# A mixture of experts on one core: token tiles of 128 rows of one expert, or of two halves of 64 rows with an expert each

## What is computed

```python
x = layernorm(x + attention(x, w_qkv, w_out))          # x: (4, 512, 256)
w, idx = top_k(softmax(x @ gate), 4); w = w / w.sum()  # gate: (256, 32)
gate_up = einsum('TD,EDF->TEF', x, gate_up_proj)       # 32 experts, (256, 192) each
g, u = split(gate_up, 2)
y = einsum('TEF,EFD->TED', u * silu(g), down_proj)     # (96, 256) each
x = layernorm(x + (y * router_weights).sum(experts))   # only the 4 chosen count
```

## Time and profile before

| | us |
|---|---|
| median of 3 runs | 473.64 (470.53 to 474.44) |
| the profiled execution | 470.53, its span 468.8 |
| PE busy | 401.1 (86%) |
| DVE, ACT, POOL busy | 281.8, 245.8, 244.0 |
| expert stage on PE | from 283.95 to 428.55 |

### The profile page before, as it was taken

One profiled execution on the slowest core, in us unless ns is written; L12 is line 12 of the kernel. 1 busy time (PEld: TensorE's weight loads), 2 busy tenths in 40 slices (PEclk: granted clock), 3 DMA queues, 4 the chain that ended last, 5 costly groups with the idle time before them and its releaser, 6 DMA issues.

```text
span 468.8 us, 9779 instructions
## 1 busy us (share of the span) xinstructions
PE 401.1 (86%) x2613; PEld 268.1 (57%) x2613; DVE 281.8 (60%) x835; ACT 245.8 (52%) x594; POOL 244.0 (52%) x362
## 2 busy tenths in 40 slices
PE   5755899999988899978988717979999999996692
PEld 2422565455564356544544416859889998984240
DVE  1225774787459985899797394534555555551295
ACT  1412265676454676558757143544666666654054
POOL 4301242533332387635874737777777667765341
PEclk9989899999999999999999876998999999999697
DMA  4689473385467157497557249979755556300993
GB/s 161 148 173 174 125 130 88 92 147 100 108 186 143 27 105 163 131 215 193 172 157 212 93 138 300 286 229 307 205 162 176 155 169 171 110 3 4 395 383 116
DMA packets 55795, 76.77 MB, mean 164 GB/s; under 512 B 9650, under 2 KB 47804, under 8 KB 54208
## 3 DMA queue, kind: packets, MB, share of 16 engines
q1 hardware_dynamic: 48112, 59.22, 49.0%
q0 software_dynamic: 7632, 16.93, 10.1%
HBM read 46.23 MB, written 33.75 MB: 171 GB/s over the span
## 4 chain that ended last, share of the span: by engine, by line
PE 56%; DVE 17%; DMA 9%; SPq 6%; issue 6%; POOL 4%; ACT 1%; ACTq 0%; DVEq 0%; POOLq 0%
PE PS L730 11%; PE PS L746 7%; PE PS L602 6%; PE PS L535 6%; PE PS L559 5%; DVE MX L989 5%; PE PS L581 4%; PE PS L717 4%; SPq L495 3%; POOL scratch_slots L1300 2%; DMA scratch_qk<-PA 2%; PE PS L546 2%; PE PS L563 2%; PE PS L740 2%; PE PS L660 2%
## 5 line engine op out<-in xcount | busy, mean ns | idle before, releaser
L845 ACT ACTIVATE PT<-PS 128x512 f32<-128x512 f32 x160 | 92.9, 596 | 49.2 <-PE PS L581 44.2
L1307 POOL DMA_INDIRECT scratch_y<-Y,XG x95 | 93.6, 985 | 36.8 <-ACT Y L899 25.1
L989 DVE TENSOR_REDUCE MX<-PS 128x1 f32<-128x384 f32 (+1 forms) x192 | 88.5, 503 | 37.1 <-PE PS L563 37.0
L1283 POOL TENSOR_SCALAR_AFFINE_SELECT PT<-PT 128x256 f32<-128x256 f32 (+1 forms) x140 | 50.9, 372 | 75.9 <-ACT PT L845 74.0
L1300 POOL DMA_INDIRECT scratch_slots<-XP,RI x64 | 63.1, 986 | 35.9 <-DVE XP L1118 19.0
L730 PE MATMUL PS<-W,XGT 128*128 x380 | 80.5, 336 | 0.3 <-DVE XGT L1204 0.2
L559 PE MATMUL PS<-KS,QS 96*128 96x512 bf16 (+3 forms) x256 | 61.6, 303 | 21.1 <-DVE MX L989 12.5
L730 PEld LDWEIGHTS PS<-W,XGT 128*128 128x128 f32 x380 | 61.8, 196 | 1.0 <-issue 0.9
L581 PE MATMUL PS<-QS,KS 98*128 98x512 bf16 (+3 forms) x256 | 60.9, 299 | 1.4 <-ACT PT L845 1.4
L1211 DVE SCALAR_TENSOR_TENSOR HH<-PS,XG,SG 128x96 f32<-128x96 f32 x95 | 30.2, 318 | 52.5 <-ACT SG L887 52.0
L746 PE MATMUL PS<-W,HT 96*128 x190 | 57.3, 383 | 0.0
(11 more groups left out here) (169 smaller groups left out, 552.9 us busy)
## 6 DMA issues: line engine op xcount, KB each, us to landing
XG<-scratch_slots SPq DMA_DIRECT2D x95, 130.0 KB, 2.7
YL<-scratch_y SPq DMA_DIRECT2D x16, 512.0 KB, 10.7
scratch_qk<-PA SPq DMA_DIRECT2D x48, 128.0 KB
KS<-scratch_qk SPq DMA_DIRECT2D x48, 128.0 KB, 7.2
W<-_L_ffn_gate_up_proj_dram SPq DMA_DIRECT2D x16, 288.0 KB, 3.6
scratch_slots<-pad SPq DMA_DIRECT2D x33, 130.0 KB, 7.4
QS<-scratch_qk SPq DMA_DIRECT2D x8, 384.0 KB, 5.0
W<-in_L_ffn_down_proj_dram SPq DMA_DIRECT2D x8, 288.0 KB, 5.6
```

Of the source, the lines that this page charges most:

```text
L845: e.activation(PT[:, p % NPT, n, :], PS[:, 2 + (rank[u] - 1) % 2, :], ACT.Exp).then_inc(st_exp, 1)
L989: t = e.tensor_reduce(M[:, h, qt:qt + 1], PS[:, kk, c0:c0 + w], AX.X, ALU.max)
L1283: e.affine_select(out=d, in_=d, compare_op=ALU.is_ge, fill=0.0, base=0, pattern=[[0, 1 if n < 2 else 2], [1, 128]], channel_multiplier=-1) ...
L1307: e.indirect_dma_start(out=YK[:, :], out_offset=bass.IndirectOffsetOnAxis(ap=XG[:, j % NXG, D + 1:D + 2].bitcast(I32), axis=0), in_=Y[:, j ...
```

## The change

A tile now has two halves of 64 slots, each with an expert of its own. The first half uses columns 0 to 63 of the array and writes PSUM partitions 0 to 63, the second half the other 64. An expert's rows are rounded up to 64, and the count becomes `TILES` = (8192/64 + 32)/2 = 80, with `EARLY` = 32. The first half's weights are still addressed in `W` by a register. Those of the second half are copied into two fixed rings: DVE copies gate and up (384 columns) into `WG`, ACT the down weights (256 columns) into `WD`. Both engines read the expert's place from the table for it. SP loads a tile with two DMAs of 64 rows and reads two tables. The fills have 64 rows. They are cut into groups of four, and behind each group stand three or two early tile loads. PE no longer drains its pipeline between early and late tiles: `experts` is one loop, and the wait for the late table moves into it. The tables lie in `WOT`, whose first content is dead by then. Row blocks of `X` are normalised on every second tile instead of every fourth.

```diff
-TILES = B * S * TOPK // 128 + NE - 1
+HALF = 64
+TILES = (B * S * TOPK // HALF + NE) // 2
-EARLY = -(-((B - 1) * S * TOPK - 127 * NE) // 128)
+EARLY = -(-((B - 1) * S * TOPK - (HALF - 1) * NE) // HALF) // 2
+FILLS = 4
...
-    plan += [("early",)]
+    plan += [("early", 0, 8)]
     plan += [("rows", B - 1, q, k) for q in range(2) for k in range(TOPK)]
-    plan += [("fill",)]
+    tile = 8
+    for n in range(0, NE, FILLS):
+        step = 3 if n < NE // 2 else 2
+        plan += [("fill", n), ("early", tile, tile + step)]
+        tile += step
+    plan.append(("early", tile, EARLY))
...
-                e.dma_start(XG[:, j % NXG, :], XS[bass.ds(slot[j], 128), :]).then_inc(xg_in[j % NXG], 16)
+                for n in range(2):
+                    if j in row_starts:
+                        slot.update(zip([(t, n) for t in row_starts[j]],
+                                        row_values(mybir.EngineType.SP, table_piece(0, n, row_starts[j]))))
+                    e.dma_start(XG[HALF * n:HALF * n + HALF, j % NXG, :],
+                                XS[bass.ds(slot[j, n], HALF), :]).then_inc(xg_in[j % NXG], 16)
...
             def stage_b(j):
                 if j >= 2:
                     e.wait_ge(hh_out, j - 1)
                 e.wait_ge(xgt_out, j + 1)
+                e.wait_ge(wg_out, j + 1)
                 for c in range(2):
-                    t = e.matmul(PS[:, 2 + j % 2, 0:2 * FF], XGT[:, j % 2, c, :],
-                                 W[:, bass.ds(reg[j] + 2 * FF * c, 2 * FF)], start=(c == 0), stop=(c == 1))
+                    e.matmul(PS[0:HALF, 2 + j % 2, 0:2 * FF], XGT[:, j % 2, c, 0:HALF],
+                             W[:, bass.ds(reg[j] + 2 * FF * c, 2 * FF)], start=(c == 0), stop=(c == 1))
+                    t = e.matmul(PS[HALF:128, 2 + j % 2, 0:2 * FF], XGT[:, j % 2, c, HALF:128],
+                                 WG[:, j % 2, 2 * FF * c:2 * FF * c + 2 * FF], start=(c == 0), stop=(c == 1))
...
-                e.matmul(PS[:, 6 + j % 2, 0:D], HT[:, j % 2, :], W[0:FF, bass.ds(reg[j] + 4 * FF, D)],
+                e.wait_ge(wd_out, j + 1)
+                e.matmul(PS[0:HALF, 6 + j % 2, 0:D], HT[:, j % 2, 0:HALF], W[0:FF, bass.ds(reg[j] + 4 * FF, D)],
+                         start=True, stop=True)
+                e.matmul(PS[HALF:128, 6 + j % 2, 0:D], HT[:, j % 2, HALF:128], WD[0:FF, j % 2, :],
                          start=True, stop=True).then_inc(y_full, 1)
...
+            def copy_down(j):
+
+                if j == EARLY:
+                    e.wait_ge(tile_at, 3)
+                if j in row_starts:
+                    reg.update(zip(row_starts[j], row_values(mybir.EngineType.Activation,
+                                                             table_piece(1, 1, row_starts[j]), (NE - 1) * WROW)))
+                if j >= 2:
+                    e.wait_ge(y_full, j - 1)
+                e.activation(WD[0:FF, j % 2, :], W[0:FF, bass.ds(reg[j] + 4 * FF, D)], ACT.Copy).then_inc(wd_out, 1)
...
-            to_normalise = {EARLY + 8 + 4 * t: t for t in range(NT)}
+            to_normalise = {EARLY + 8 + 2 * t: t for t in range(NT)}
...
+            def copy_up(j):
...
+                if j >= 2:
+                    e.wait_ge(gu_full, j - 1)
+                e.tensor_copy(WG[:, j % 2, :], W[:, bass.ds(reg[j], 4 * FF)]).then_inc(wg_out, 1)
+
+            def experts():
+                copy_up(0)
+                for i in range(TILES + 1):
+                    if i < TILES:
+                        stage_a(i)
+                    if i:
+                        stage_b(i - 1)
+                    if i + 1 < TILES:
+                        copy_up(i + 1)
```

More of the change, by code:

```diff
@@ L390, in build, with table_piece, by_half @@
                       for lo in range(first, end, TOGETHER)}
-        def table_piece(row, tiles):
-            table, first = (ETI, 0) if tiles[0] < EARLY else (TI, EARLY)
-            return table[row:row + 1, tiles[0] - first:tiles[-1] + 1 - first]
+        def table_piece(row, half, tiles):
+            table, first, n = (ETI, 0, EARLY) if tiles[0] < EARLY else (TI, EARLY, TILES - EARLY)
+            at = half * n - first
+            return table[row:row + 1, at + tiles[0]:at + tiles[-1] + 1]
+        def by_half(table):
+            return table.rearrange("p (n j) -> p j n", n=2)
         def row_values(engine, row, most=NE * CAP):
@@ L483, in _ @@
                 elif kind == "early":
[L484 to L488, removed]
+                    lo, hi = a
+                    if lo == 0:
+                        e.wait_ge(*free(("etable",)))
+                        for q in range(4):
+                            wait_rows(e, B - 1, q)
+                        wait_pv(e, PAIRS - 1)
+                    for j in range(lo, hi):
                         load_tile(j)
                 elif kind == "fill":
+                    n, = a
                     e.wait_ge(fill_at, 1)
                     wait_const(e, "pad")
-                    for n in range(0, NE, 4):
-                        for v in row_values(mybir.EngineType.SP, FI[0:1, n:n + 4]):
-                            e.dma_start(XS[bass.ds(v, 128), :], pad[:, :]).then_inc(fill_out, 16)
+                    for v in row_values(mybir.EngineType.SP, FI[0:1, n:n + FILLS]):
+                        e.dma_start(XS[bass.ds(v, HALF), :], pad[0:HALF, :]).then_inc(fill_out, 16)
             e.wait_ge(tile_at, 3)
@@ L1213, in stage_b, with experts @@
                                        op1=ALU.mult).then_inc(hh_out, 1)
[L1215 to L1217 removed]
+            reg = {}
+            def copy_up(j):
+                if j == EARLY:
+                    e.wait_ge(tile_at, 3)
+                if j in row_starts:
+                    reg.update(zip(row_starts[j], row_values(mybir.EngineType.DVE, table_piece(1, 1, row_starts[j]),
+                                                             (NE - 1) * WROW)))
+                if j >= 2:
+                    e.wait_ge(gu_full, j - 1)
+                e.tensor_copy(WG[:, j % 2, :], W[:, bass.ds(reg[j], 4 * FF)]).then_inc(wg_out, 1)
+            def experts():
+                copy_up(0)
+                for i in range(TILES + 1):
+                    if i < TILES:
                         stage_a(i)
[L1219 removed]
+                    if i:
                         stage_b(i - 1)
[L1222 to L1223 removed]
+                    if i + 1 < TILES:
+                        copy_up(i + 1)
+            e.wait_ge(*free(("etable",)))
+            e.wait_ge(w_in, 48 * kinds["w"])
+            experts()
             for t in range(0, NT + 2, 2):
```

75 lines of the change are left out of this document (36 added, 39 removed).

## The result

The changed kernel takes **505.78 us** (median of 4 runs, 505.55 to 506.04) against 473.28 us before (4 runs on the same chip): ratio 1.0696, 95% interval 1.0649 to 1.0743. The forecast was 484, its range 472 to 500. Slower is right, and so is the main reason, but the time is 22 us over the forecast and outside the range. The profiled execution is one of 505.85 us with a span of 504.0. (In the prediction, rows 10 and 11 are cited the wrong way round: the landing time is in rows 10, POOL's first scatter in rows 11.)

A forecast was written before the change was run, and what follows sets the result against it. The expert stage was taken as bound by columns streamed through PE's array. Tiles -21.2, gap and second start -5.65, visits +37.9 gave +11.0 us on the median 473.64: 484.6, given as 484, range 472 to 500.

The forecast's parts named there:

- The tiles removed: On PE in the expert stage: fifteen tiles fewer at 1.416 us each, 21.2 us saved.
- the halves run side by side: Stages b and d on PE: column strips run together, so a pair of halves costs the price of one.
- the rival of 571 us: Stages b and d on PE: halves run one after the other, +1.08 us a tile, 86 us in all; chance 0.02.
- The switch is not free: Against the rival on PE that switching costs nothing for halves of 64: period 1.42, 453 to 465 us, chance 0.16.
- The copies are hidden: Weight copies on DVE and ACT: done an iteration before PE needs them, costed at nothing.
- DVE and ACT keep up: Per tile, DVE needs at most 1.38 us and ACT 1.28 to 1.58, plus 0.07 each, under PE's 1.89.
- the second start of the pipeline: PE between early and late tiles: one loop removes the 2.05 us gap and 3.6 for a second start, 5.65 together.
- the new period is 1.416 + 0.47 = 1.89 us: PE, per tile: two visits to column tiles at 0.235 us each added to the old period; 37.9 us in 80 tiles.
- weights are not hidden: Rival on PE: each of six passages a tile exposes 0.06 us, 0.36 a tile, 29 us; 490 to 515 us, chance 0.10.
- so nothing waits: SP's queue: at 0.58 us a load and 0.665 a fill, rows land before PE wants them, so the 5.65 us are gained.
- The margin of 10 us: Tile 17's rows: landed by 310 us, wanted by PE at 320.
- the test itself: Sign of error: PE waiting for DMAs of XG between 300 and 340 us would mean SP binds.

The follow-up runs named there:

- experiment 1: The kernel before with its 95 tiles, only stages b and d cut into two column tiles of 64, nothing copied: 549.51 us against 518.0.
- experiment 5: The changed kernel with the fills issued by ACT, 128 rows each, so that SP only loads tiles: 487.97 us, ratio 1.0388 to the kernel before.
- the pairs: The changed kernel with two tiles per visit and fills on ACT's queue: ratio 0.9889; with c and d two tiles later still, 462.64 us, ratio 0.9832.
- experiment 4: The changed kernel with c ahead of b, one visit per tile: 513.89 us, ratio 0.9970; with tiles loaded before fills as well, 483.42 us, ratio 1.0270.
- experiment 2: The kernel before with each tile load of 128 rows cut into two DMAs of 64: 529.43 us against 518.0, ratio 1.0288.

## Why the prediction missed

**Right.** The tiles removed are worth 1.416 us each and the halves run side by side (the rival of 571 us is out). The switch is not free: 0.095 us on entry into stage b and 0.101 on exit, where the forecast had 0.097. The copies are hidden: experiment 1 has the same period without them. DVE and ACT keep up; the second start of the pipeline is gone. With what the forecast left out taken away, its own sum comes back: experiment 5 gives a stage of 164.0 us against 155.6, and 8.6 of the difference are the period's.

**The step "the new period is 1.416 + 0.47 = 1.89 us"** has the right mechanism and too small a size. The price of a visit was read from strips of 32 columns: 0.235, of which 0.194 are entry and exit and 0.041 the rest. At full clock the median steps of one tile are longer than before by 0.095 us into stage b, 0.049 from its first record to its second, 0.101 out of it, 0.135 into d, 0.047 inside d, 0.102 out of it, and 0.052 from a's first transpose to its second. These are all of the 0.581 us. So the rest is about 0.05 twice in a visit: from its first record to its second, and behind the first full-width matmul after it (for c, which has only one, it shows as 0.135 instead of 0.095). Three orders of PE give the same price: (1.997 - 1.416)/2 = 0.290, 1.713 - 1.416 = 0.297, and 2 x (1.560 - 1.416) = 0.288 us per visit. The forecast had 0.235. That is 8.6 us in 80 tiles. The rival "weights are not hidden" was right in kind at most for the first record and not for every passage: the later steps in stage b are 0.162 us, in the pairs too, as before. The measured time lies in its band of 490 to 515, but for another reason: it asked for 0.36 us a tile beyond the forecast, and there are 0.107. The Trainium skill (TensorE: Matmul & The Clock Gate, LDWEIGHTS) gives a load as its columns over 1.2 GHz, 53 ns for 64; the 0.047 to 0.049 inside a visit are near it, and the later passages, at 0.162, show no such load. By this rule of the Trainium skill, as an estimate, 128 columns would be 107 ns and 96 columns 80, while the step behind a visit is 0.052 with 128 and 0.040 with 96. So that the two steps are exposed weights is plausible but not shown. (That loads overlap matmuls only for another row group, as the forecast quotes, the page says under The mechanism, and the steps of 0.162 between matmuls on the same 128 rows do not bear it out.)

**The step "so nothing waits"** failed. It took 0.58 us for a load of 64 rows from a row of loads with 128 rows. The record is 0.469 us instead of 0.333, and with the tables' reads a DMA took 0.81 on average, so tile 17 came 8 us later than forecast. It also put all 4.4 us of the stage's start and draining ahead of the tiles, while TensorE took the first 17 tiles in 34.0 us and stood at tile 17 at 315.9 instead of 320. The margin of 10 us became a wait of 2.5. The forecast had drawn up the test itself (a wait for `XG` between 300 and 340: SP binds), but gave it no price and no rival. The 5.2 us of waits are the small part of it.

**What the prediction never weighed** is the clock behind a wait. The row that shows it stood in the profile of before: its one gap of 2.05 us has a dip of the clock behind it, of 3.4 us. At half speed that costs at most 1.7 us. In the changed kernel two such gaps cost 16.3, the largest part of the miss. Experiment 5 shows that they are the cause, not the column tiles alone.

**Open** is why the clock comes back late. Behind a gap, kernels with no, one or half a visit per tile have it back after 3.1 to 6.1 us of work. With two visits per tile it took 16.6, 20.1, 17.1, 23.2, 12.1, 26.4, 17.4, 13.9 and 42.1 us, but 3.4 and 4.8 in two cases, and at the very start of the stage 4.7 to 6.1 in the five of them on undisturbed chips. Nor does the clock fall behind every gap: waits of 3.0 and 2.5 us in experiment 4, with one visit per tile, were followed by no dip. What differs between the long, the short and the missing dips the traces do not show.

## What to carry to other kernels

When matmuls are cut into column tiles, count the changes between full width and tiles in TensorE's order and put all tiled work of an iteration side by side; with two iterations together the price halves again. Count DMAs and not bytes in an issuing queue, and take their price from a row of the same shape: half the rows cost more than all of them here. Give every expected wait of TensorE ahead of dense work a second price for the clock behind it (here between nothing and 41.0 x 0.435 = 18 us), and read the count of matmuls in a window, since busy time hides the loss.

## What the runs showed of the hardware

- A load of 64 rows occupies SP for 0.469 us, one of 128 rows of the same 1040 bytes for 0.333 (median records of the two kernels, and 0.468 in experiment 2); the fills show it too (0.518 against 0.332).
- A visit from full-width float32 matmuls to two column tiles of 64 and back costs 0.29 us at full clock beyond its columns, whether one, two or four stages lie in it.
- Around an idle gap of some 2 us the granted clock can fall to the lower of its two levels and stay there for 3.4 to 41 us, though TensorE is busy behind the gap; behind other such gaps it does not fall.
